# A four-stage decoder layer on one core: where the mixer's product of B and C, its scans and its residual stand, and where the attention's statistics do

## The reference

```python
x = layernorm(x + mixer_and_gated_mlp(x))      # rmsnorm, Mamba2 mixer, rmsnorm, gated MLP
x = layernorm(x + cross_attention(x, ctx))     # 16 heads of 32, softmax over 256 context rows
x = layernorm(x + quantised_mlp(x))            # relu, hidden width 2048, fp8 grid

# mixer: z, xBC, dt = split(u @ in_proj); xBC = silu(conv4(xBC) + conv_b); x, B, C = split(xBC)
# dt = softplus(dt + dt_bias); h = h * exp(dt * A) + dt * B x;  y = h C + D x      (per head, over time)
# out = rmsnorm(y * silu(z)) @ out_proj
```

## Time and profile before

| | us |
|---|---|
| median of 3 runs | 2718.32 |
| lowest, highest | 2716.38, 3430.97 |
| the profiled execution's own time | 2718.93 |
| its span in the trace | 2717.1 |
| PE, DVE, ACT, POOL busy | 2662.6, 1521.5, 1019.4, 692.7 |
| of the chain that ended last: PE, DVE, issue | 89%, 7%, 2% |

### The profile page before, as it was taken

How to read it: one execution, slowest core, us unless ns; L and a number is a source line. 1 busy time by engine, 2 the same in 40 slices (tenths; PEclk the granted TensorE clock), 3 DMA queues, 4 the chain that set the end, 5 groups by cost and what they waited for, 6 DMA issues and landing times.

```text
span 2717.1 us, 42369 instructions
## 1 busy us (share of the span) xinstructions
PE 2662.6 (98%) x15264; PEld 2070.6 (76%) x15264; DVE 1521.5 (56%) x2561; ACT 1019.4 (38%) x2375; POOL 692.7 (25%) x594
## 2 busy tenths in 40 slices
PE   7999999999999999999999989999999999999999
PEld 5777777777778888888888867777777767777776
DVE  8787797797795322331233277777777773111122
ACT  6344334334344222122212155555555553222221
POOL 5553553553552101000100101322233322000000
PEclk9999999999999999999999999999999999999999
DMA  4001001101114101110111221110111124211111
GB/s 154 21 27 47 28 18 46 37 9 46 44 48 143 62 1 62 62 62 0 62 62 34 82 67 55 63 45 24 62 54 62 58 67 150 79 46 46 46 46 47
DMA packets 85482, 147.83 MB, mean 54 GB/s; under 512 B 4032, under 2 KB 17984, under 8 KB 85408
## 3 DMA queue, kind: packets, MB, share of 16 engines
q1 hardware_dynamic: 85408, 146.84, 15.7%
HBM read 113.27 MB, written 33.55 MB: 54 GB/s over the span
## 4 chain that ended last, share of the span: by engine, by line
PE 89%; DVE 7%; issue 2%; ACT 1%; DMA 0%; DVEq 0%; SPq 0%; POOL 0%; ACTq 0%; POOLq 0%
PE ps L75 23%; PE ps L77 23%; PE ps L76 23%; PE ps L1813 4%; PE ps L2176 4%; PE ps L816 2%; PE ps L1825 2%; PE ps L1804 2%; DVE mx_m L608 1%; DVE mx_cv L600 1%; PE ps L792 1%; PE ps L804 1%; PE ps L747 1%; PE ps L844 1%; PE ps L1756 1%
## 5 line engine op out<-in xcount | busy, mean ns | idle before, releaser
L1507 ACT ACTIVATE at_pr<-ps,at_nm 128x256 f32<-128x256 f32 x512 | 235.5, 472 | 203.8 <-DVE at_nm L1661 203.8
L1183 DVE TENSOR_TENSOR gm_m_lo<-gm_m,gm_m_hi 128x512 fp32r<-128x512 f32 (+1 forms) x88 | 60.9, 692 | 416.9 <-ACT gm_m_hi L1100 416.9
L75 PE MATMUL ps<-sh_u_hi,gm_gu_hi 128*128 128x512 f32 (+1 forms) x704 | 274.7, 390 | 0.0
L76 PE MATMUL ps<-sh_u_lo,gm_gu_hi 128*128 128x512 f32 (+1 forms) x704 | 274.6, 390 | 0.0
L77 PE MATMUL ps<-sh_u_hi,gm_gu_lo 128*128 128x512 f32 (+1 forms) x704 | 274.6, 390 | 0.0
L1667 DVE COPY at_pT<-ps 128x512 f32<-128x512 f32 x256 | 176.0, 687 | 139.7 <-PE ps L1813 137.8
L1094 ACT ACTIVATE gm_sg<-ps 128x512 f32<-128x512 f32 (+1 forms) x88 | 52.7, 598 | 517.8 <-PE ps L77 517.6
L543 POOL TENSOR_TENSOR mx_m<-mx_m,mx_g 128x512 f32<-128x512 f32 x128 | 185.4, 1449 | 86.6 <-DVE mx_m L610 86.4
L75 PE MATMUL ps<-sh_u_hi,qm_w_hi 128*128 128x512 f32 x512 | 201.4, 393 | 2.1 <-issue 1.1
L77 PE MATMUL ps<-sh_u_hi,qm_w_lo 128*128 128x512 f32 x512 | 199.4, 389 | 0.0
L76 PE MATMUL ps<-sh_u_lo,qm_w_hi 128*128 128x512 f32 x512 | 199.2, 389 | 0.0
(11 more groups left out here) (253 smaller groups left out, 6350.7 us busy)
## 6 DMA issues: line engine op xcount, KB each, us to landing
sh_xf<-x_scratch SPq DMA_DIRECT2D x16, 1024.0 KB, 7.4
mx_xr<-in_x SPq DMA_DIRECT2D x8, 1024.0 KB, 6.2
h_scratch<-mx_xr SPq DMA_DIRECT2D x8, 1024.0 KB, 5.0
sh_xf<-h_scratch SPq DMA_DIRECT2D x8, 1024.0 KB, 8.1
gm_xr<-in_x SPq DMA_DIRECT2D x8, 1024.0 KB, 7.3
gm_r<-h_scratch SPq DMA_DIRECT2D x8, 1024.0 KB, 6.2
x_scratch<-gm_r SPq DMA_DIRECT2D x8, 1024.0 KB, 5.1
at_cf<-in_ctxT SPq DMA_DIRECT2D x16, 512.0 KB, 3.7
```

Source lines behind the costliest of these rows:

```text
L75: nc.tensor.matmul(out, l_hi, r_hi, start=first, stop=False)
L76: nc.tensor.matmul(out, l_hi, r_lo, start=False, stop=False)
L1507: A(pr[h][:, t, :], SC[h][:, SEQ * t:SEQ * t + SEQ], ACT.Exp, bias=nm[:, 4 * n + h, t:t + 1], accum_out=sums[:, 2 * b + t, 4 * g + h:4 * g ...
```

## The change

In the mixer the first part of the product of B and C goes to the bank MISC, after convolution chunk 5 instead of 7, and the transposes of the decay factors stand after chunk 3 instead of 5. Scan 0 stands before convolution 6 on DVE, scans 1 and 2 and the first `scale_x` before convolution 8; chunk 9 moves into the first turn of the j loop. The output is scaled by ACT (`scale_out`, into the buffers m0) and added by POOL, in the tiles 0 to 6. ACT's squares and norms of the next tile and POOL's `first` move within the tile. In the attention only DVE's order changes: in the steps 1 to 7 one `statistics` stands between the first two copies of the slots 3 to 6, and `gather` between those of slot 7; in step 0 the weight splits stand between these copies, and `prev.norm` behind the second.

```diff
@@ -462,6 +465,14 @@
+        def scale_out(i, n):
+            t = OUT[n]
+            act.wait_ge(s["out"], KI * i + KI)
+            act.wait_ge(s["y"], KI * i + KI)
+            act.wait_ge(s["rg"], i + 1)
+            A(m0[t][:, :], ps[t][:, :], ACT.Copy, scale=rg[:, t:t + 1]).then_inc(s["ho"], 1)
         def main(i):
...
@@ -469,49 +480,60 @@
                 exp_ln(i)
+            else:
+                scale_out(i - 1, 2)
+                scale_out(i - 1, 3)
             tap(i, 1)
...
             for n in range(2, NCONV - 1):
-                if n == NCONV - 2:
+                if n == NCONV - 4:
                     act.wait_ge(s["G"], i + 1)
                     at(act, s["M"], 2 * NH * i)
-                    A(g0[:, :], BC[0][:, :], ACT.Copy).then_inc(s["Ge"], 1)
+                    A(g0[:, :], MISC[:, :], ACT.Copy).then_inc(s["Ge"], 1)
                     A(g1[:, :], BC[1][:, 0:NT // 2], ACT.Copy).then_inc(s["Ge"], 1)
-                tap(i, n)
-                silu(i, n - 1)
+                if n == NCONV - 2:
+                    zsilu(i, 0)
+                    silu(i, n - 1)
+                    tap(i, n)
+                else:
+                    tap(i, n)
+                    silu(i, n - 1)
                 if step_0(i):
                     wt.high(act, min(3 * KD + 2 * (n - 1), IN_PIECES))
-                if n >= 5:
-                    square(i + 1, n - 5)
-            silu(i, NCONV - 2)
-            zsilu(i, 0)
-            tap(i, NCONV - 1)
-            silu(i, NCONV - 1)
             for j in range(KI):
...
                     zsilu(i, j + 1)
+                    if j == 0:
+                        silu(i, NCONV - 2)
                 else:
...
                         split(i + 1, k)
+                if j in (5, 6):
+                    norm(i + 1, 2 * j - 10)
+                    norm(i + 1, 2 * j - 9)
                 act.wait_ge(s["g"], KI * i + j + 1)
...
                 if j == 0:
+                    tap(i, NCONV - 1)
                     at(act, s["ss"], i)
...
                 A(acc[:, :] if j == 0 else sq[:, :], zs[j % 2][:, :], ACT.Square).then_inc(s["gs"], 1)
-                if 1 <= j <= TT:
-                    norm(i + 1, j - 1)
+                if j == 1:
+                    silu(i, NCONV - 1)
+                if j < TT:
+                    square(i + 1, j)
                 if final(i) and j >= 1:
                 exp_ln(i + 1)
+                scale_out(i, 0)
+                scale_out(i, 1)
@@ -544,10 +565,17 @@
                     add_squares(i, (h - 3) // 2)
+                if h == 9:
+                    first(i + 1)
             add_squares(i, 7)
-            at(pool, s["h1"], TT * i)
+            at(pool, s["ho"], TT * i)
             pool.wait_ge(s["sse"], i + 1)
             G(rg[:, :], v0[:, :], mhalf[:, :], ALU.pow).then_inc(s["rg"], 1)
+            if not final(i):
+                pool.wait_ge(s["xr"], 16 * i + 16)
+            for n, t in () if final(i) else enumerate(OUT):
+                pool.wait_ge(s["ho"], TT * i + n + 1)
+                G(xr[:, t, :], xr[:, t, :], m0[t][:, :], ALU.add).then_inc(s["h1"], 1)
@@ -603,6 +631,9 @@
         def scan(i, h):
             dve.wait_ge(s["bc"], NH * i + h + 1)
+            if h == 0:
+                at(dve, s["h1"], TT * i)
             at(dve, s["y"], KI * i + h // 2 - 1)
...
@@ -680,21 +711,23 @@
                 V.memset(daT[0:2 * NH, SEQ * b:SEQ * b + 1].bitcast(F32), 0.0).then_inc(s["dac"], 1)
-            for n in range(6, NCONV - 1):
+            for n in range(5, NCONV - 1):
+                if n == 6:
+                    scan(i, 0)
+                elif n == NCONV - 2:
+                    scan(i, 1)
+                    scan(i, 2)
+                    scale_x(i, 0)
                 conv(i, n)
...
                     wt.low(dve, 3 * KD + n - 1)
-            scan(i, 0)
-            scan(i, 1)
-            scale_x(i, 0)
-            conv(i, NCONV - 1)
             if step_0(i):
...
             for j in range(KI):
-                if j + 1 < KI:
+                if j >= 2:
+                    g_low(i, j - 1)
+                if 0 < j < KI - 1:
                     scan(i, 2 * j + 2)
-                if j >= 1:
-                    g_low(i, j - 1)
                 if j == KI - 1:
...
@@ -708,6 +741,9 @@
                 V.tensor_tensor(zs[j % 2][:, :], xc[:, j, :], zs[j % 2][:, :], ALU.mult).then_inc(s["g"], 1)
+                if j == 0:
+                    g_low(i, 0)
+                    conv(i, NCONV - 1)
                 if final(i) and 2 <= j <= 5:
...
@@ -721,10 +757,12 @@
                 dt_second(i + 1)
-            dve.wait_ge(s["out"], KI * i + KI)
-            dve.wait_ge(s["xr"], 16 * i + 16)
-            dve.wait_ge(s["rg"], i + 1)
-            for t in range(TT):
+            if final(i):
+                dve.wait_ge(s["out"], KI * i + KI)
+                dve.wait_ge(s["xr"], 16 * i + 16)
+                dve.wait_ge(s["rg"], i + 1)
+            for t in range(TT) if final(i) else ():
                 V.scalar_tensor_tensor(xr[:, t, :], ps[t][:, :], rg[:, t:t + 1], xr[:, t, :], ALU.mult,
...
@@ -764,17 +802,17 @@
         def conv_in(i, n, also=None):
...
                 pe.wait_ge(*wt.lows(n // 4 * KD + 2 * KD - 1))
+            if 2 <= n <= 5:
+                at(pe, s["ho"], TT * (i - 1) + n - 1)
             if n >= 4:
                 pe.wait_ge(s["cv"], 3 * NCONV * i + 3 * (n - 3))
-            elif n == 2:
-                at(pe, s["h1"], TT * i)
             project(CB[n], E_X + P * CH[n], also).then_inc(s["in"], 1)
         def z_in(i, c):
...
             if c == 0:
-                pe.wait_ge(s["a"], i + 1)
+                pe.wait_ge(s["Ge"], 2 * i + 2)
             elif c < 3:
...
@@ -798,8 +836,9 @@
                 pe.wait_ge(s["dac"], 3 * i + 3)
+            elif h == 1:
                 pe.wait_ge(s["Ge"], 2 * i + 2)
-            elif h >= 2:
+            else:
                 pe.wait_ge(s["sc"], NH * i + h - 1)
...
@@ -859,35 +898,40 @@
                 conv_in(i, 0)
-            for n in range(1, 6):
+            for n in range(1, 4):
                 conv_in(i, n)
...
             last.then_inc(s["dat"], 1)
-            for n in range(6, NCONV - 2):
+            for n in range(4, 6):
                 conv_in(i, n)
+            pe.wait_ge(s["a"], i + 1)
             at(pe, s["sc"], NH * i)
...
                 o = SEQ * b
-                T.matmul(BC[0][:, o:o + SEQ], bT[:, o:o + P], cT[:, o:o + SEQ], start=True, stop=True)
+                T.matmul(MISC[:, o:o + SEQ], bT[:, o:o + P], cT[:, o:o + SEQ], start=True, stop=True)
                 last = T.matmul(BC[1][:, P * b:P * b + P], bT[:, o + P:o + SEQ], cT[:, o + P:o + SEQ], start=True, stop=True)
             last.then_inc(s["G"], 1)
+            spread(i, 0)
+            for n in range(6, NCONV - 2):
+                conv_in(i, n)
+            spread(i, 1)
+            z_in(i, 0)
+            spread(i, 2)
             conv_in(i, NCONV - 2)
-            z_in(i, 0)
-            spread(i, 0)
-            spread(i, 1)
-            conv_in(i, NCONV - 1)
             turn_x(i, 0)
-            spread(i, 2)
+            spread(i, 3)
+            z_in(i, 1)
             for j in range(KI):
-                if j + 1 < KI:
+                if 0 < j < KI - 1:
                     z_in(i, j + 1)
                     spread(i, 2 * j + 3)
-                else:
+                elif j == KI - 1:
                     turn(i + 1, 0)
...
@@ -896,10 +940,12 @@
                     turn(i + 1, 3)
+                if j == 0:
+                    conv_in(i, NCONV - 1)
+                else:
+                    chunk_out(i, j - 1)
                 if j + 2 < KI:
                     spread(i, 2 * j + 4)
-                if j >= 1:
-                    chunk_out(i, j - 1)
             if final(i):
...
@@ -1700,7 +1746,16 @@
                 take_pT(i, n, 0)
+                if step_0(i):
+                    if n < TT:
+                        wt.low(dve, 13 + n)
+                elif 3 <= n < 7:
+                    statistics(i - 1, n - 3, before(i, n + 2) + 1)
+                elif n == 7:
+                    gather(i - 1)
                 take_pT(i, n, 1)
+                if step_0(i) and n < TT:
+                    prev.norm(dve, NP - 1, n)
                 if n == 0 and not step_0(i):
...
@@ -1714,18 +1769,6 @@
                     take(i, 2 * n + 1)
-                if step_0(i) and n < TT:
-                    wt.low(dve, 13 + n)
-                    prev.norm(dve, NP - 1, n)
-                if not step_0(i):
-                    if n == 3:
-                        statistics(i - 1, 0, before(i, 5) + 1)
-                    elif n == 4:
-                        for t in range(1, 3):
-                            statistics(i - 1, t, before(i, 5 + t) + 1)
-                    elif n == 5:
-                        statistics(i - 1, 3, before(i, 8) + 1)
-                        gather(i - 1)
```

(6 more changed lines are left out.)

## The result

| | us |
|---|---|
| after, median of 6 runs | 2779.01 (2775.49 to 2780.37) |
| before, median of 6 runs | 2718.47 |
| ratio to before, 95% interval | 1.0221 (1.0208 to 1.0234) |
| span of the profiled execution, before and after | 2717.1 and 2777.7 |

The account below looks back on a forecast made before the run. TensorE, busy 98% of the span, was taken to bound the kernel. Mixer -10, attention's copies -5, six waits +52, their clock +9.6 and attention's end +14 summed to +60.6: 2779 us, 2774 to 2790 (eight in ten: 2752 to 2800).

Parts of the forecast that it names:

- mixer: Mixer's new order: -11.2 in steps 1 to 6, 0 in step 0, +1 in step 7; together -10, between -13 and -4.
- statistics and splits between the copies: Attention: both waits for VectorE's copies gone, -3.4 in six steps, about -2 in steps 0 and 7; together -5.
- six waits for xf: Attention steps 2 to 7: TensorE's transposes wait for the later load of xf, 9.9 + 5 x 8.4 = +52 us.
- their clock: Behind each wait for xf, eight matmuls 0.43 apart instead of 0.23: 1.6 us each, +9.6 for six.
- end of the attention: Step 7: later `gather` delays the MLP's next weights, `take_rT` and TensorE's L1838; +14 us, between +3 and +17.
- The queue: SyncE's queue in the attention: xf's load stands behind store and residual's load; shift 14.6, slack 4.7, then 6.2.
- Rival (a): Attention: the waits for xf come without the half clock, or with a part of it; 2768 us, chance 0.22.
- The margin of 0.4 us: Mixer's j = 2: TensorE's 8.28 us against VectorE's 7.8 to 7.9 before z's third projection; missing by 0.3 gives -9.
- my walk: Mixer step 0: earlier transposes and first spread wait about 2 us each for the softplus chain, third z 1.3.
- (b): Attention: load lands in 5 to 6 us or transposes start later, waits 2 to 3 shorter; 2764 or 2757, chance 0.15.
- (c): Attention: load of xf not behind the store, so only the gains are left; 2704 us, 0.6% faster, chance 0.05.
- (d): Mixer: margin missed each turn or GpSimd's additions hold up scans; +17 in place of -10, 2806 us, chance 0.10.

## Why the prediction was right

| term | forecast | found | from |
|---|---|---|---|
| mixer | -10 | -9.6 | first gate matmul; alone 2709.43 |
| gated MLP | 0 | +0.4 | first gate matmul to the attention's first |
| statistics and splits between the copies | -5 | -6.6 | steps 0 to 6 less their waits and clock; alone -6.3 |
| six waits for xf | +52 | +50.6 | sum of the waits |
| their clock | +9.6 | +14.0 | distance of the transposes |
| end of the attention | +14 | +11.8 | the last step and what follows it, less the sixth wait and its clock |
| sum | +60.6 | +60.6 | spans |

Every mechanism was there, in its place, but the exact agreement of the sum is luck of about 5 us: the clock cost 4.4 more, the mixer and the gated MLP 0.8, and the waits, the attention's gain and its end together 5.2 less.

- **The queue.** The step on which the forecast stood was that the load of xf, which needs nothing of `gather`, stands behind a store that does. The load moved to another queue shows it, and `gather` alone in the kernel before repeats it. The slack was read right within 1.6 us: waits of 9.9 and 8.4 were forecast, 8.29 and 8.45 came. The first was overrated since I carried the landing of 8.4 us over to the later issue; it was 7.1 after. This isn't scatter: this load took 8.4 to 8.7 in all five traces with `gather` in slot 5 and 7.0 to 7.2 in the seven with `gather` in slot 6 or 7 and the load in SyncE's queue. Why it lands faster when it is issued later no run shows.
- **The clock.** I took eight slow matmuls per wait, from the one stretch in the earlier trace rows. The six stretches differ from 1.3 to 2.8 us. The rule of the Trainium skill that I weighed ("TensorE: Matmul & The Clock Gate", "HAM oscillation — how this bites in real kernels") held: all six waits for a DMA were followed by the lower clock; behind the first the granted clock was 0.50. Rival (a), without that cost, falls.
- **The attention's gain.** I summed the idle time that the rows show (0.56 a step); the step got shorter by 1.02. By the windows view the idle time was 0.68, and TensorE's busy time fell too, from 81.08 to 80.74, for the same matmuls. My reading, which no run shows, is that a delay of a matmul behind its operand is partly counted as busy. That was the term of my sum that was undersized.
- **The end.** I forecast 12.0 plus 1.6 of clock plus 0.5. The wait is 11.41 with 2.3 of clock behind it (from L1881 to the first matmul of the MLP's second weights 36.43 us, where it was 34.16), 13.7 together. The term is 11.8 since two waits of 1.11 and 1.03 earlier in that step are all but gone. They are gone with `gather` in slot 6 too and largely stay when `gather` alone moves, where the end costs 13.3: so they are a gain of the new order that I hadn't counted, and not waits that the long one replaces.
- **The mixer.** The margin of 0.4 us ahead of z's third projection held, and the six steps give 10.8, where 11.2 was forecast. The new wait of the last step came (2.05, forecast up to 2.5) with 1.6 of clock that I hadn't counted, so that step is 2.0 longer instead of 1, and step 0 kept waits of 1.73, 2.52 and 1.48, near the 2, 2 and 1.3 of my walk.
- **Rivals (b), (c) and (d)** fall: the waits were 8.3 to 8.6 and not 2 to 3 us less, the load stayed behind the store, and no mixer step of the loop got longer.

## What to carry to other kernels

When an instruction moves on an engine with time to spare, follow what it releases to the end, past each in-order queue; here four instructions of 0.37 us in all cost 75 us, because a load that had nothing to do with them stood behind the store that had. Slack is used up without a sign and then costs one for one: 5.4 us of shift cost nothing, 9.4 cost 3 a step, 14.6 cost 8.4, and each of these waits took lost clock with it. A step's length between two equal instructions is the better measure of a small gain than its idle rows.

## What the hardware showed beside this

**Small VectorE instructions that end only with the GpSimd one beside them.** In the kernel whose load comes from ScalarE's queue, two rows of VectorE and two of GpSimd:

```profile
1757.69 0.88 DVE L1731 CAST at_r_hl<-at_rinv 128x16 fp32r<-128x16 f32 x1
1758.61 1.22 DVE L1733 TENSOR_TENSOR at_r_hl<-at_rinv,at_r_hl 128x16 fp32r<-128x16 f32 x1
```
```profile
1753.53 5.01 POOL L1668 TENSOR_TENSOR at_r<-at_r,at_cols 128x512 f32<-128x512 f32 x4 [8.71 <-DMA at_r<-x_scratch]
1758.50 1.29 POOL L1650 TENSOR_TENSOR at_o_lo<-at_o,at_o_hi 128x512 fp32r<-128x512 f32 x1
```

In all but seven places of the trace the same two take 0.15 to 0.47 and 0.17 to 0.20. Each ends when GpSimd's instruction does, at 1758.5 and 1759.8. The Trainium skill ("SBUF — State Buffer", "SBUF: two separate sides") says that a VectorE operation in a mode with two ports and a GpSimd operation exclude each other for a whole instruction, and so do one with two SBUF inputs and a GpSimd operation that reads SBUF. The second row of VectorE, with two SBUF inputs, agrees; for the cast no row shows its mode. Right behind the two stands VectorE's projection (L1690) that the profile names for TensorE's wait of 0.61 to 0.85 a step of that run. With `gather` in slot 5 the last step shows it again: VectorE's two weight splits and the division's split lie beside GpSimd's additions.

```profile
2224.26 1.21 DVE L1726 TENSOR_TENSOR at_r_hl<-at_rinv,at_r_hl 128x16 fp32r<-128x16 f32 x1
2225.40 2.37 DVE L225 TENSOR_TENSOR qm_w_lo<-qm_stage,qm_w_hi 128x512 fp32r<-128x512 f32 x2
```
```profile
2221.68 5.53 POOL L1661 TENSOR_TENSOR at_r<-at_r,at_cols 128x512 f32<-128x512 f32 x4
```

Two such splits take 1.3 alone, and GpSimd's four additions, 5.01 above, take 5.53 here. The wait of 1.64 follows. That these overlaps cause the two waits is read from the rows; no run kept GpSimd away from them, so it isn't shown by an edit.

**The same wait, with and without lost clock.** Waits of 2.28 and 2.29 us at one place of the program were followed by full clock in one execution and by half in another. Ten us behind the wait of 2.28 of the earlier trace rows the kernel before has one of 2.17 that I overlooked, and behind that the same group is slow:

```profile
1630.14 1.93 PE L1825 MATMUL ps<-at_pT,at_v 128*32 128x256 f32 x16 [2.17 <-DVE at_pT L1667]
```

Waits of 1.83 to 2.05 in the mixer's last step did it in two executions of seven. A price per wait from one profile is good to about a factor of two: over the six waits of 8 us it ran from 1.3 to 2.8.
